# The second experts' weights: one transfer of 12 KB runs a tile in place of three of 2 KB and 1 KB runs

## The chip, the cores and the metric

One core of one Trainium2 chip. The metric is the device time of the whole program in microseconds (us); the kernel before was run three times, and its median is 5924.18 us.

## The reference, cut to what matters

A tower of feed-forward blocks with routed experts and of attention blocks, on 4096 tokens of width 256. The change touches only the second kind of feed-forward block, which occurs twice (`_L1_ffn_ref`). Each token goes to the one expert of 32 whose gate is highest, scaled by that gate's sigmoid:

```python
def _L1_ffn_ref(hidden_states, gate_w, ..., routed_gate_w, routed_up_w, routed_down_w):
    H, I, E = 256, 512, 32
    x = hidden_states.reshape(-1, h)
    shared_out = _swiglu(x, shared_gate_w, shared_up_w, shared_down_w)
    logits = x @ gate_w
    topk_ids = jnp.argmax(logits, axis=-1)
    scores = jax.nn.sigmoid(jnp.max(logits, axis=-1))[:, None]
    xs = x * scores
    ...
    g = _grouped_mm(sorted_x, routed_gate_w, tokens_per_expert)
    u = _grouped_mm(sorted_x, routed_up_w, tokens_per_expert)
    d = _grouped_mm(jax.nn.silu(g) * u, routed_down_w, tokens_per_expert)
    ...
    return (shared_out + routed_out).reshape(b, s, h)
```

An expert has a gate and an up matrix of 256 x 512 and a down matrix of 512 x 256, all float32: 512 KB each, 1.5 MB (1.573 million bytes) together.

## The kernel before, in words

The program runs its blocks one after another, with a barrier between them: first experts (names that begin with a), attention (b), first experts again (c), second experts (d), another attention (e), second experts again (f). A block of second experts has three phases: a norm (dn, fn), a routing phase (dr, fr) that computes the shared expert and lays out the tokens, and the experts' phase (de, fe) in `experts1_phase`, which alone uses the code that is changed.

Routing puts the tokens into NS1 = 4096/128 + 32 = 64 slots of 128 rows, each slot for one expert; unused rows and slots point to dummy rows. `experts1_phase` runs over these 64 tiles. Every engine has its own program, and semaphores tie them together; a name such as `s_y` counts the tiles that have come so far.

- SyncE (`tile`, L944): reads the tile's expert number from `eid`, waits until the tile four earlier has gone through its down product (`s_y`, lag WR = 4), and issues the three loads of that expert's matrices (L949 to L951) into slot `u % WR` of `wg`, `wu` and `wd`. Each load adds 16 to the slot's semaphore `s_w`. In `wg` and `wu` a partition holds 2 rows (HC = 2) of 512 floats, which are 2 KB runs in DRAM; in `wd` it holds 4 rows (FC = 4) of 256 floats, 1 KB runs.
- GpSimd (L960 to L987): issues the indirect gathers of the tiles' rows, six tiles ahead (LEAD = RING - 2), and the indirect scatters of the results. Its order per tile n is written out: gather n + 6, wait for the result's copy (`s_yc`), wait until the scatter of tile n - 1 has landed (`s_o`, L984), scatter n (L985). So scatters never overlap each other, and a gather stands behind the scatter of the tile before.
- VectorE: scales the gathered rows into `gs` (L1058), and multiplies silu(gate) by up into `h` (L1067).
- TensorE (`tile`, L1007): transposes tile n + 1 (L1010, helper at L995), waits for the weights of tile n (L1011), the 16 gate and the 16 up products of 128x128 by 128 columns (L1017), then the 8 matmuls of 256 columns of the down product of tile n - 1 (L1003).
- ScalarE: copies the transposed rows out of PSUM (L1032), silu (L1045), and copies the result into one of four `y` buffers (L1038); a buffer is free when the scatter four tiles earlier has landed.

SyncE's loads and GpSimd's gathers and scatters run on the same 16 DMA engines, through two queues: q1 (SyncE) and q0 (GpSimd). After the last tile SyncE waits for all scatters and reads the routed rows back (`r`, L957), and VectorE adds them to x.

The loads and the wait for them are:

```python
for dst, src in ((wg, "L1_rg"), (wu, "L1_ru"), (wd, "L1_rd")):
    sp.dma_start(dst[:, u % WR], D[src][ds(e, 1)].rearrange("e (c p) f -> p (e c) f", p=P)
                 ).then_inc(s_w[u % WR], 16)
...
pe.wait_ge(s_w[u % WR], 48 * quarter(k, u))
```

The first experts' phases (ae, ce) load each expert's matrices in one transfer of 3 KB a partition (`L0_w`, L684).

Of the kernel before, what the change touches and what calls it, by code (L numbers as in the profile page):

```python
# [16 lines left out]
P = 128  # L17
B, S, H = 2, 2048, 256
# [5 lines left out]
HC = H // P  # L24
EPS = 1e-5
NEG_BIG = -3.0e38
ds = bass.ds
# [6 lines left out]
E1, F1 = 32, 512  # L34
# [27 lines left out]
def rings_of(eng, count, body, ring=RING, start=0):  # L62

    i0, i1 = start // ring, count // ring
    for u in range(ring):
        body(start + u, u, i0 + 1, start + u, None)
    if i1 - i0 > 2:
        with eng.Fori(i0 + 1, i1 - 1) as i:  # L70
            for u in range(ring):
                body(i * ring + u, u, i + 1, None, None)
    for u in range(ring):
        body(count - ring + u, u, i1, None, ring - u)


def after(eng, sem, n, lag, first, count=lambda k: k):

    if first is None or first >= lag:
        eng.wait_ge(sem, count(n - lag + 1))  # L80


def moved(first, d):

    return None if first is None else first + d
# [818 lines left out]
WR = 4  # L904
# [6 lines left out]
def experts1_phase(nc, name, D, C, x, stats, rows, routed, eid, idx, ident, s_g, s_o, run):  # L911
# [3 lines left out]
    g0, o0 = run * 16 * (NS1 // RING), run * 16 * (NS1 // NY1)  # L915
    FC = F1 // P
    with Scope(nc, name) as sc:
        wg, wu = (sc.sb(n, [P, WR, HC, F1]) for n in ("wg", "wu"))
        wd = sc.sb("wd", [P, WR, FC, H])
        g = sc.sb("g", [P, RING, ROW1])  # L920
        gs = sc.sb("gs", [P, 4, H])
        xe = sc.sb("xe", [P, 2, HC, P])
# [1 line left out]
        h = sc.sb("h", [P, 2, FC, P])  # L924
# [3 lines left out]
        psG = sc.ps("psG", [P, 2, FC, P])  # L928
        psU = sc.ps("psU", [P, 2, FC, P])
        psY = sc.ps("psY", [P, 2, BLK])  # L930
        s_w = [sc.sem(f"w{u}") for u in range(WR)]
# [4 lines left out]
        s_gs, s_xt, s_xe, s_gp, s_up, s_sg, s_hh, s_y, s_yc = (  # L936
            sc.sem(n) for n in ("gs", "xt", "xe", "gp", "up", "sg", "hh", "y", "yc"))

        quarter = lambda k, u: k * (RING // 4) + (u // 4 + 1 - RING // 4)

        with nc.Block() as block:  # L941

            @block.sync
            def _(sp):  # L944
                def tile(n, u, k, first, last):
                    e = sp.value_load(eid[0:1, ds(n, 1)], min_val=0, max_val=E1 - 1)

                    after(sp, s_y, n, WR, first)
                    for dst, src in ((wg, "L1_rg"), (wu, "L1_ru"), (wd, "L1_rd")):  # L949
                        sp.dma_start(dst[:, u % WR], D[src][ds(e, 1)].rearrange("e (c p) f -> p (e c) f", p=P)  # L950
                                     ).then_inc(s_w[u % WR], 16)  # L951

                rings_of(sp, NS1, tile)
                for u in range(NY1):
                    sp.wait_ge(s_o[u], o0 + 16 * (NS1 // NY1))
                for q in range(NQ1):
                    sp.dma_start(r[:, q * (NT // NQ1) * H:(q + 1) * (NT // NQ1) * H].rearrange("p (t h) -> p t h", h=H),  # L957
                                 routed[q * (T // NQ1):(q + 1) * (T // NQ1), :].rearrange("(t p) h -> p t h", p=P)
                                 ).then_inc(s_r[q], 16)
# [29 lines left out]
            @block.tensor  # L989
            def _(pe):  # L990
                def transposes(n, u, first):
                    pe.wait_ge(s_gs, n + 1)
                    after(pe, s_xe, n, 2, first)
                    for c in range(HC):
                        last = nc.tensor.transpose(psX[:, u % 2, c * P:(c + 1) * P],  # L995
                                                   gs[:, u % 4, c * P:(c + 1) * P], ident[:])
                    last.then_inc(s_xt, 1)

                def down(n, u, first):
                    pe.wait_ge(s_hh, n + 1)  # L1000
                    after(pe, s_yc, n, 2, first)
                    for m in range(FC):
                        last = nc.tensor.matmul(psY[:, u % 2, 0:H], h[:, u % 2, m, :], wd[:, u % WR, m, :],  # L1003
                                                start=(m == 0), stop=(m == FC - 1))
                    last.then_inc(s_y, 1)

                def tile(n, u, k, first, last):  # L1007

                    if last != 1:
                        transposes(n + 1, (u + 1) % RING, moved(first, 1))  # L1010
                    pe.wait_ge(s_w[u % WR], 48 * quarter(k, u))  # L1011
                    pe.wait_ge(s_xe, n + 1)
                    after(pe, s_hh, n, 2, first)
                    for ps, w, done in ((psG, wg, s_gp), (psU, wu, s_up)):
                        for m in range(FC):
                            for c in range(HC):
                                mm = nc.tensor.matmul(ps[:, u % 2, m, :], w[:, u % WR, c, m * P:(m + 1) * P],  # L1017
                                                      xe[:, u % 2, c, :], start=(c == 0), stop=(c == HC - 1))
                        mm.then_inc(done, 1)
                    if first != 0:  # L1020
                        down(n - 1, (u - 1) % RING, moved(first, -1))

                transposes(0, 0, 0)
                rings_of(pe, NS1, tile)
                down(NS1 - 1, RING - 1, None)

            @block.scalar
# [1062 lines left out]
def macaron_kernel(nc, D, out):  # L2090
# [10 lines left out]
    with Scope(nc, "all") as sc:  # L2101
# [23 lines left out]
        def experts1(n, run):  # L2125
            with Scope(nc, n) as f:
                idx, eid, dest = f.sb("idx", [P, NS1], I32), f.sb("eid", [P, NS1], I32), f.sb("dest", [P, NT], I32)
                with Scope(nc, n + "f") as g:
                    xnT, logits = g.sb("xnT", [P, HC, T]), g.sb("logits", [P, NT * E1])
                    wg, wu, wd = g.sb("wg", [P, HC, F1]), g.sb("wu", [P, HC, F1]), g.sb("wd", [P, F1 // P, H])  # L2130
                    s_w = g.sem("w")
                    loads = (wg[:], D["L1_sg"]), (wu[:], D["L1_su"]), (wd[:], D["L1_sd"])
                    norm_phase(nc, n + "n", x, stats, xnT, C["ident"], rows1, ROW1, D["L1_gate"], E1, logits, loads, s_w)
                    route1_phase(nc, n + "r", D, C, x, xnT, logits, rows1, eid, idx, dest, wg, wu, wd, s_w)
                experts1_phase(nc, n + "e", D, C, x, stats if run == 0 else None, rows1, routed, eid, idx, C["ident"], s_g1, s_o1, run)
# [44 lines left out]
def by_chunk(a):  # L2180

    return a.reshape(-1, P, a.shape[-1]).transpose(1, 0, 2)


def lay_out(I):
    D = {"L0_x": I["L0_attn_x"].reshape(T, H)}
    D["L0_gate"] = by_chunk(I["L0_ffn_gate_weight"].T)
    D["L0_ebias"] = I["L0_ffn_e_bias"]
    for k, n in (("sg", "shared_gate"), ("su", "shared_up"), ("sd", "shared_down")):
        D["L0_" + k] = by_chunk(I["L0_ffn_" + n].T)  # L2190
    up = [I["L0_ffn_" + n].transpose(0, 2, 1).reshape(E0, HC, P, F0).transpose(0, 2, 1, 3).reshape(E0, P, HC * F0)
          for n in ("w1", "w3")]
    D["L0_w"] = np.concatenate(up + [I["L0_ffn_w2"].transpose(0, 2, 1)], 2)
    for n in "qkv":
        D["L0_w" + n] = by_chunk(I["L0_attn_W" + n].T)
    D["L0_bqk"] = np.concatenate([I["L0_attn_b" + n].reshape(HC, P).T for n in "qk"], 1)
    D["L0_bv"] = I["L0_attn_bv"]
    wo = np.zeros((NHEAD, VW, H), np.float32)
    wo[:, :DH] = I["L0_attn_Wo"].T.reshape(NHEAD, DH, H)
    wo[0, DH] = I["L0_attn_bo"]  # L2200
    D["L0_wo"] = by_chunk(wo.reshape(NHEAD * VW, H))
    D["L1_gate"] = by_chunk(I["L1_ffn_gate_w"])
    for k, n in (("sg", "shared_gate_w"), ("su", "shared_up_w"), ("sd", "shared_down_w")):
        D["L1_" + k] = by_chunk(I["L1_ffn_" + n])
    for k, n in (("rg", "routed_gate_w"), ("ru", "routed_up_w"), ("rd", "routed_down_w")):
        D["L1_" + k] = I["L1_ffn_" + n]
    for n in ("q1", "q2", "k1", "k2", "v", "c"):
        D["L1_w" + n] = by_chunk(I["L1_attn_W" + n])
    heads = (np.arange(P) // (2 * VW))[:, None] + 2 * (np.arange(B * NHEAD // 2) % (NHEAD // 2))[None, :]
    D["L1_lam"] = np.stack([I["L1_attn_" + n][heads].reshape(P, -1) for n in ("lq1", "lq2", "lk1", "lk2")], 1)  # L2210
    D.update(constants())
    return {n: np.ascontiguousarray(a) for n, a in D.items()}
# [15 lines left out]
```

## Time and profile before

| what | value |
|---|---|
| three runs | 5935.9, 5924.18, 5909.79 us (median 5924.18) |
| span of the profiled execution, the only time given of it | 5916.1 us, mean granted TensorE clock 0.916 |
| TensorE matmul, weight load | 5058.1 us (85%), 2711.9 us (46%) |
| VectorE, ScalarE, GpSimd | 57%, 43%, 31% |
| DMA | 659.28 MB, mean 111 GB/s; SyncE's queue q1 27.0% of 16 engines, GpSimd's q0 13.2% |
| loads of the second experts | 64 a phase and matrix, 512.0 KB each; gate 4.7 and 4.9, up 5.9 and 5.9, down 7.3 and 7.5 us to landing (de, fe) |

Busy times are shares of the whole span and of stages with different limits. "To landing" is from the start of the issuing instruction to the last of its completions. DMA shares are the time that packets took, as a share of 16 engines in the window asked for.

### The profile page before, as it was taken

What the parts mean: (1) busy time and instruction counts of PE and PEld (TensorE: products, weight loads), DVE (VectorE), ACT (ScalarE), POOL (GpSimd) and SP (SyncE); (2) the same over time, 40 slices, a digit from 0 to 9 for tenths busy, and PEclk for the clock granted to TensorE, in tenths of its full rate; (3) what the DMA queues carried; (4) which work ended last, traced back from release to release, by engine and by line L of the source; (5) the groups of instructions that cost most, each with busy time, mean ns of one, the idle gap of its engine ahead of it and who ended that gap; (6) DMA issues with size and microseconds to landing.
All of it is one profiled execution on the core that took longest, in us unless ns stands there. A gap on an engine that the chain in (4) does not pass through costs nothing. (4 is left out here: it accounts for less than half of the span.)

```text
span 5916.1 us, 82750 instructions
## 1 busy us (share of the span) xinstructions
PE 5058.1 (85%) x29088; PEld 2711.9 (46%) x29088; DVE 3390.4 (57%) x6345; ACT 2567.7 (43%) x5102; POOL 1828.3 (31%) x1800
## 2 busy tenths in 40 slices
PE   6566489999978566499987999999999999799996
PEld 3455333333325455357973333333333333255896
DVE  7511468887846721241119788878888878343111
ACT  2311217776662311132215176766766766513221
POOL 2388311111101288534331122222222222104332
PEclk9778779999989687699998899999999999889998
DMA  3476561222213277606986411221221221120798
GB/s 107 116 148 149 138 171 33 62 58 68 62 53 104 76 156 151 149 26 212 330 269 198 108 37 40 63 49 40 64 47 40 64 48 40 55 69 1 267 318 268
DMA packets 503528, 659.28 MB, mean 111 GB/s; under 512 B 147310, under 2 KB 358318, under 8 KB 497998
## 3 DMA queue, kind: packets, MB, share of 16 engines
q1 hardware_dynamic: 370158, 500.99, 27.0%
q0 software_dynamic: 133056, 154.15, 13.2%
q8 instruction: 192, 3.15, 0.2%
q14 instruction: 122, 1.00, 0.1%
HBM read 489.33 MB, written 164.20 MB: 110 GB/s over the span
## 5 line engine op out<-in xcount | busy, mean ns | idle before, releaser
L1724 DVE TENSOR_REDUCE ea_mx<-ea_psA 128x1 f32<-128x512 f32 (+3 forms) x2304 | 1373.9, 653 | 242.0 <-PE ea_psA L1585 144.1
L1706 ACT ACTIVATE ea_pr<-ea_psB 128x512 f32<-128x512 f32 (+3 forms) x2560 | 1198.9, 535 | 567.4 <-PE ea_psB L1608 557.7
L1585 PE MATMUL ea_psA<-ex_kx,ex_qx 99*128 99x512 bf16 (+3 forms) x2560 | 868.4, 357 | 20.2 <-DVE ea_mx L1724 13.3
L1608 PE MATMUL ea_psB<-ex_qx,ex_kx 99*128 99x512 bf16 (+3 forms) x2560 | 846.2, 349 | 0.0
L1724 DVE TENSOR_REDUCE ba_mx<-ba_psA 128x1 f32<-128x512 f32 (+3 forms) x1152 | 686.2, 653 | 144.3 <-PE ba_psA L1585 95.6
L1706 ACT ACTIVATE ba_pr<-ba_psB 128x512 f32<-128x512 f32 (+3 forms) x1280 | 601.5, 536 | 288.9 <-PE ba_psB L1611 155.5
L1625 PE MATMUL ea_psO<-ea_pr,ea_vx 128*32 128x512 f32 (+3 forms) x5120 | 603.5, 543 | 20.9 <-POOL ea_pr L1554 14.0
L1585 PEld LDWEIGHTS ea_psA<-ex_kx,ex_qx 99*128 99x128 bf16 x2560 | 250.3, 98 | 551.8 <-DVE ea_mx L1724 427.8
L1585 PE MATMUL ba_psA<-bx_kx,bx_qx 108*128 108x512 bf16 (+3 forms) x1280 | 443.5, 364 | 7.8 <-PEq L1146 4.5
L1608 PE MATMUL ba_psB<-bx_qx,bx_kx 108*128 108x512 bf16 (+3 forms) x1280 | 424.9, 349 | 14.6 <-DMA bx_qx<-ba_mT 14.4
L1608 PEld LDWEIGHTS ea_psB<-ex_qx,ex_kx 99*128 99x128 bf16 x2560 | 246.5, 98 | 310.3 <-ACT ea_pr L1706 141.0
L1554 POOL TENSOR_SCALAR_AFFINE_SELECT ea_pr<-ea_pr 128x512 f32<-128x512 f32 x256 | 162.7, 638 | 633.7 <-ACT ea_pr L1706 633.5
L1625 PE MATMUL ba_psO<-ba_pr,ba_vx 128*32 128x512 f32 (+3 forms) x2560 | 300.3, 541 | 2.1 <-ACT ba_osb L1696 2.1
L1542 POOL DMA_DIRECT2D ex_qx<-ea_mT x192 | 106.8, 563 | 485.3 <-DVE ea_mT L1746 485.3
L1585 PEld LDWEIGHTS ba_psA<-bx_kx,bx_qx 108*128 108x128 bf16 x1280 | 126.0, 99 | 280.6 <-DVE ba_mx L1724 207.5
L716 POOL DMA_INDIRECT acc<-ce_y,c_idx x128 | 204.8, 1600 | 43.7 <-issue 36.0
L716 POOL DMA_INDIRECT acc<-ae_y,a_idx x128 | 204.4, 1597 | 43.9 <-issue 35.3
L1625 PEld LDWEIGHTS ea_psO<-ea_pr,ea_vx 128*32 128x32 f32 x5120 | 102.2, 108 | 242.6 <-ACT ea_pr L1706 183.5
L1588 PE MATMUL ea_psA<-all_cb 128*128 128x128 bf16 x1024 | 206.1, 225 | 0.0
L793 DVE TENSOR_TENSOR ae_h<-ae_sg,ae_psH 128x256 f32<-128x256 f32 x64 | 26.9, 421 | 302.2 <-ACT ae_sg L774 302.2
L793 DVE TENSOR_TENSOR ce_h<-ce_sg,ce_psH 128x256 f32<-128x256 f32 x64 | 26.9, 421 | 299.8 <-ACT ce_sg L774 299.8
L1608 PEld LDWEIGHTS ba_psB<-bx_qx,bx_kx 108*128 108x128 bf16 x1280 | 123.9, 98 | 139.3 <-ACT ba_pr L1706 59.5
(528 smaller groups left out, 8260.9 us busy)
## 6 DMA issues: line engine op xcount, KB each, us to landing
de_wg<-in_L_rg SPq DMA_DIRECT2D x64, 512.0 KB, 4.7
de_wu<-in_L_ru SPq DMA_DIRECT2D x64, 512.0 KB, 5.9
de_wd<-in_L_rd SPq DMA_DIRECT2D x64, 512.0 KB, 7.3
fe_wg<-in_L_rg SPq DMA_DIRECT2D x64, 512.0 KB, 4.9
fe_wu<-in_L_ru SPq DMA_DIRECT2D x64, 512.0 KB, 5.9
fe_wd<-in_L_rd SPq DMA_DIRECT2D x64, 512.0 KB, 7.5
ae_w<-in_L_w SPq DMA_DIRECT2D x64, 384.0 KB, 3.6
ce_w<-in_L_w SPq DMA_DIRECT2D x64, 384.0 KB, 3.8
```

The lines of the kernel that those rows point to most:

```text
L716: nc.gpsimd.indirect_dma_start(out=acc[a], out_offset=column(n, a), in_=y[:, n % RING, a, :], in_offset=None, bounds_check=bound, oob_is_e ...
L793: nc.vector.tensor_tensor(h[:, u % 2, :], sg[:, u % 2, :], psH[:, u % 2, 1, :], ALU.mult).then_inc(s_hh, 1)
L1542: pool.dma_start(qx[MR:MR + 3, s, hh, t0 * P:(t0 + tc) * P].rearrange("l (t q) -> l t q", q=P), mT[hh * 3 * tc:(hh + 1) * 3 * tc, k, :]).t ...
L1554: nc.gpsimd.affine_select(own, own, [[0, HV], [1, P]], ALU.is_ge, 0.0, base=0, channel_multiplier=-1).then_inc(s_pm, 1)
L1585: last = nc.tensor.matmul(psA[:, slot, at:at + n], qx[0:KB, s, hh, t * P:(t + 1) * P], kx[0:KB, s, hh, k:k + n], start=True, stop=not diag)
L1588: last = nc.tensor.matmul(psA[:, slot, at + n - P:at + n], C["identb"], C["maskA"], start=False, stop=True)
L1608: last = nc.tensor.matmul(psB[:, slot, off:BLK], kx[0:KB, s, hh, kt * P:(kt + 1) * P], qx[0:KB, s, hh, Q * BLK + off:(Q + 1) * BLK], start ...
L1625: last = nc.tensor.matmul(psO[hh * VW:(hh + 1) * VW, off:BLK], vx[:, s, kt, vcol:vcol + VW], pr[:, j % 4, hh, off:BLK], start=(kt == 0), s ...
L1706: nc.scalar.activation(pr[:, j % 4, hh, off:BLK], psB[:, exp_slot(n), off:BLK], ACT.Exp).then_inc(s_exp, 1)
L1724: v.tensor_reduce(out, src, AX.X, ALU.max).then_inc(s_ar, 1)
```

## The change

The host lays an expert's three matrices out side by side: for each expert and partition 3072 floats (12 KB), first the two rows of the gate matrix, then the two of the up matrix, then the four of the down matrix. In SBUF the three tensors `wg`, `wu` and `wd` become views of one tensor `w` of the same size. SyncE issues one transfer per tile, and TensorE waits for 16 per load in place of 48. Nothing else differs.

```diff
-        wg, wu = (sc.sb(n, [P, WR, HC, F1]) for n in ("wg", "wu"))
-        wd = sc.sb("wd", [P, WR, FC, H])
+        w = sc.sb("w", [P, WR, 3 * HC * F1])
+        at = lambda u, part: w[:, u, part * HC * F1:(part + 1) * HC * F1]
+        wg, wu = ([at(u, part).rearrange("p (c f) -> p c f", c=HC) for u in range(WR)] for part in range(2))
+        wd = [at(u, 2).rearrange("p (m h) -> p m h", m=FC) for u in range(WR)]
...
-                    for dst, src in ((wg, "L1_rg"), (wu, "L1_ru"), (wd, "L1_rd")):
-                        sp.dma_start(dst[:, u % WR], D[src][ds(e, 1)].rearrange("e (c p) f -> p (e c) f", p=P)
-                                     ).then_inc(s_w[u % WR], 16)
+                    sp.dma_start(w[:, u % WR], D["L1_w"][ds(e, 1)].rearrange("e p f -> p (e f)")).then_inc(s_w[u % WR], 16)
...
-                        last = nc.tensor.matmul(psY[:, u % 2, 0:H], h[:, u % 2, m, :], wd[:, u % WR, m, :],
+                        last = nc.tensor.matmul(psY[:, u % 2, 0:H], h[:, u % 2, m, :], wd[u % WR][:, m, :],
...
-                    pe.wait_ge(s_w[u % WR], 48 * quarter(k, u))
+                    pe.wait_ge(s_w[u % WR], 16 * quarter(k, u))
...
-                    for ps, w, done in ((psG, wg, s_gp), (psU, wu, s_up)):
+                    for ps, own, done in ((psG, wg, s_gp), (psU, wu, s_up)):
...
-                                mm = nc.tensor.matmul(ps[:, u % 2, m, :], w[:, u % WR, c, m * P:(m + 1) * P],
+                                mm = nc.tensor.matmul(ps[:, u % 2, m, :], own[u % WR][:, c, m * P:(m + 1) * P],
...
-    for k, n in (("rg", "routed_gate_w"), ("ru", "routed_up_w"), ("rd", "routed_down_w")):
-        D["L1_" + k] = I["L1_ffn_" + n]
+    rows = [I["L1_ffn_routed_" + n].reshape(E1, -1, P, I["L1_ffn_routed_" + n].shape[-1]).transpose(0, 2, 1, 3).reshape(E1, P, -1)
+            for n in ("gate_w", "up_w", "down_w")]
+    D["L1_w"] = np.concatenate(rows, 2)
```

## Rows read from the trace of the kernel before

**Rows 1.** Chain that ended last, phase fe: start us, us, what.
```profile
5514.97 1.79 PE fe_psG L1017 x16
...
5520.49 1.79 PE fe_psG L1017 x16
...
5631.50 6.65 DMA routed<-fe_y,f_idx
5638.94 4.88 DMA routed<-fe_y,f_idx
...
5829.42 5.11 DMA routed<-fe_y,f_idx
```
**Rows 2.** Waits from 5500 to 5910 us: waiter, releaser, us, times, longest.
```profile
POOL routed L985 <- DMA routed<-fe_y,f_idx: 203.9, 59, 6.4
...
PE fe_psX L995 <- DVE fe_gs L1058: 22.4, 11, 10.9
```
**Rows 3.** Windows: length, busy us of PE, PEld, DVE, ACT, POOL; clock, DMA, GB/s.
```profile
2730.00:2780.00 50.00, 50.00 (x383) 47.70 (x382) 10.00 (x20) 11.35 (x28) 15.75 (x16) 1.00 0.99 334
...
2980.00:3030.00 50.00, 48.76 (x370) 45.42 (x370) 9.29 (x19) 11.69 (x27) 17.50 (x18) 1.00 0.95 314
...
5680.00:5730.00 50.00, 47.78 (x355) 44.16 (x354) 8.84 (x18) 10.73 (x26) 18.19 (x18) 1.00 0.97 317
```
**Rows 4.** Line L985 (the scatters) from 5630 to 5835 us.
```profile
DMA to landing us min/median/max: 4.0/5.0/6.6
```
**Rows 5.** Timeline, scatters and last result copies: start us, us, engine, line.
```profile
3088.80 0.37 ACT L1038 COPY de_y<-de_psY 128x256 f32<-128x256 f32 x1 [2.92 <-PE de_psY L1003]
...
3095.38 0.98 POOL L985 DMA_INDIRECT routed<-de_y,d_idx  x1 [2.19 <-DMA routed<-de_y,d_idx]
...
5520.97 1.04 POOL L985 DMA_INDIRECT routed<-fe_y,f_idx  x1 [12.09 <-ACT fe_y L1038]
...
5874.73 0.37 ACT L1038 COPY fe_y<-fe_psY 128x256 f32<-128x256 f32 x1 [2.92 <-PE fe_psY L1003]
...
5879.53 0.98 POOL L985 DMA_INDIRECT routed<-fe_y,f_idx  x1 [2.20 <-DMA routed<-fe_y,f_idx]
5882.70 0.98 POOL L985 DMA_INDIRECT routed<-fe_y,f_idx  x1 [2.19 <-DMA routed<-fe_y,f_idx]
```
**Rows 6.** DMA queues from 5530 to 5850 us: packets, MB, share of 16 engines.
```profile
q1 hardware_dynamic: 60541, 88.66, 81.9%
q0 software_dynamic: 5177, 14.17, 15.3%
```
**Rows 7.** DMA queue q1 from 236 to 245 us: loads of 3 KB runs (ae_w).
```profile
q1 hardware_dynamic: 961, 2.65, 81.2%
```
**Rows 8.** DMA queue q1 from 1755 to 1764 us: a store of 8 KB rows (yT).
```profile
q1 hardware_dynamic: 144, 1.05, 28.4%
```
**Rows 9.** DMA queue q1 from 3520 to 3530 us: loads of 8 KB rows (ea_rec).
```profile
q1 hardware_dynamic: 192, 1.05, 45.6%
```
**Rows 10.** Timeline, first gate products of tiles 1 and 63 in de and fe.
```profile
2729.80 1.95 PE L1017 MATMUL de_psG<-de_xe,de_wg 128*128 128x128 f32 x16
...
3083.30 1.95 PE L1017 MATMUL de_psG<-de_xe,de_wg 128*128 128x128 f32 x16
...
5514.81 1.95 PE L1017 MATMUL fe_psG<-fe_xe,fe_wg 128*128 128x128 f32 x16
...
5869.23 1.95 PE L1017 MATMUL fe_psG<-fe_xe,fe_wg 128*128 128x128 f32 x16
```
**Rows 11.** Timeline, the start of phase de: first loads, the second gather.
```profile
2715.58 0.42 SPq L950 DMA_DIRECT2D de_wg<-in_L_rg  x1
...
2716.60 0.42 SPq L950 DMA_DIRECT2D de_wd<-in_L_rd  x1
2717.04 1.06 POOL L969 DMA_INDIRECT de_g<-rows,d_idx  x1 [0.30 <-issue]
2717.80 0.38 SPq L950 DMA_DIRECT2D de_wg<-in_L_rg  x1
```

## The prediction

> **What bounds the kernel now.** I read the page first, then the chain of waits, then the two stages that the change touches, by waits, windows, timeline and DMA share. TensorE is busy 85% of the span on the page, but that is an average over stages; the edit is used only in the two stages of the second experts, "de" (2715 to 3119 us) and "fe" (5499 to 5902 us). There are 64 tiles in each, so what matters is what sets a tile's time there.
>
> Early in a stage it is TensorE: a window of 50 us holds 50.00 us of matmul [rows 3], and the chain runs through the gate, up and down products, one tile each 5.52 us (5514.97 to 5520.49) [rows 1]. Later the chain leaves TensorE: from 5631.50 to 5829.42 it is made of 35 scatters of results, one behind the other [rows 1], because GpSimd waits for the landing of scatter n-1 before it issues scatter n (L984 to L985): 59 such waits, 203.9 us [rows 2]. TensorE feels it through the gathers, which stand in the same GpSimd program: 11 waits for gathered rows, 22.4 us, of which 10.9 is the stage's start [rows 2]. The matmul share of a 50 us window falls to 47.78 in fe and 48.76 in de [rows 3].
>
> What makes a scatter slow is the weight traffic. Beside the loads it lands in a median of 5.0 us (4.0 to 6.6) [rows 4]; at the stage's end, with no load left, scatters follow each other every 3.17 us (5879.53, 5882.70) [rows 5]. GpSimd needs 0.79 us from a landing to the next start: 5631.50 + 6.65 = 5638.15, and the next begins at 5638.94 [rows 1]. So a scatter alone takes 3.17 - 0.79 = 2.38 us, and 5.0 - 2.38 = 2.62 us is waiting behind weights. The period of the chain is 5.0 + 0.79 = 5.79 us by the median; from the first scatter at 5520.97 to the last at 5882.70 there are 63 steps of 5.74 [rows 5]. The stage loses because 5.74 is just above TensorE's 5.52, and by no more.
>
> The 16 DMA engines stand at the same brim. In 320 us of fe the weight queue takes 81.9% and GpSimd's 15.3% [rows 6]. Weights: 0.819 x 16 x 320 / 88.66 = 47.3 engine-us per MB; a tile of 1.573 MB is 74.4, over 16 engines 4.65 us. GpSimd's: 88.66 / 1.573 = 56.4 tiles, 0.153 x 320 / 56.4 = 0.87 us. Together 5.52 us a tile: full.
>
> **The change, part by part.**
>
> *Run length.* The same bytes, but 128 pieces of 12 KB in place of 512 of 2 KB and 512 of 1 KB. No row shows 12 KB. The nearest by route are the first experts' loads, 3 KB a partition into 128 partitions: 0.812 x 16 x 9 / 2.65 = 44.1 engine-us per MB [rows 7], so 4.34 us a tile. The nearest by size are stores of 8 KB rows: 0.284 x 16 x 9 / 1.05 = 38.9 [rows 8], so 3.83 us. I take 3.95, nearer the second, since what a piece costs shrinks with their count, and keep 3.83 and 4.34 for the range. Farthest are loads of 8 KB rows: 0.456 x 16 x 10 / 1.05 = 69.5 [rows 9], 6.83 us a tile; with GpSimd's 0.87 that is 7.70, and 126 steps would cost 126 x (7.70 - 5.74) = 247 us. Those go into 32 partitions each (L1500 to L1502), the weights into 128 as the 3 KB loads do, so I keep that end out of the range. The Trainium skill ("DMA: Bandwidth & Descriptors", Where 436 GB/s comes from) puts the ceiling of the 16 engines at 435 GB/s; an estimate by that page is 1.573 MB / 435 GB/s = 3.62 us, by which the start below would cost 0.7 us a stage less and the time would be 1.3 us lower.
>
> *What follows for the chain.* A drain of 3.95 in place of 4.65 shortens the wait behind it by 0.70: landing 4.3, period 4.3 + 0.79 = 5.09, below 5.52. With 4.34 it is 4.69 + 0.79 = 5.48, barely below. The DMA engines then have 5.52 - 3.95 - 0.87 = 0.70 us a tile to spare. In both cases TensorE's 5.52 holds to the end, and TensorE is late next. Worth in the middle: de's tile 1 starts at 2729.80 and its tile 63 at 3083.30, fe's at 5514.81 and 5869.23 [rows 10]. That is 353.50 and 354.42 for 62 tiles; 62 x 5.52 = 342.24. Gain 11.26 + 12.18 = 23.4 us.
>
> *Tail.* The last scatters run late because the chain lags. Without a lag tile 62's scatter starts when its copy ends, 5874.73 + 0.37 = 5875.10, and the last 3.17 later at 5878.27; now it is 5882.70: 4.4 us. In de 3088.80 + 0.37 + 3.17 = 3092.34 against 3095.38: 3.0 [rows 5]. Gain 7.4 us.
>
> *Start.* TensorE transposes tile 1 before tile 0's products (L1010, L1017), so the stage begins when gather 1 lands. Now gather 1 (2717.04) is issued before tile 1's first transfer (2717.80), behind tile 0's load alone [rows 11]. SyncE needs 1.20 us from tile 0's last issue (2716.60) to tile 1's first; with one issue a tile, tile 1's whole load goes out at 2715.58 + 1.20 = 2716.78, before gather 1. Gather 1 then waits for one load more, 3.95, less the 0.70 by which the first is shorter: 3.2 us a stage, a loss of 6.4 in all. Its ends: nothing, if the gather is served between pieces, and 4.34 each.
>
> *At nothing:* SyncE issues one transfer a tile and not three, off the path between tiles. The wait for 16 in place of 48 asks for the same bytes; a load is issued three tiles (16.6 us) before its use, and the view of [rows 2] lists no wait of TensorE for weights. If that cover went, a drain of 3.95 would stand in the open at each tile. The matmuls keep count and shape and read other addresses of the same partitions. The array in DRAM is laid out on the host.
>
> **Sum.** 23.4 + 7.4 - 6.4 = 24.4 us less than the profiled span of 5916.1 gives 5891.7. That span is 8.1 below the median of the three runs (5924.18), so by the median 5899.8 us, 0.41% faster. A measurement of this kernel can tell about 0.5% from no change; the three runs spread over 26 us.
>
> **Rivals.**
> A. *No start cost*: the gather slips between pieces. 23.4 + 7.4 = 30.8, so 5893.4. For it: few pieces are queued when the first gathers come. Against it: beside loads, GpSimd's transfers wait 2.62 us now.
> B. *Little shortens.* The weights' 4.65 us hold stalls beside gathers that may go by time and not by piece; the 3 KB loads at 44.1 against 47.3 show a gain of 7% for twice the run. If the landing falls by just 0.1, that is 63 x 0.1 x 2 = 12.6, less 6.4: 5918.
> C. *The scatter meets a whole load.* All 1.5 MB now enter the queue at once, where before three transfers came 0.5 us apart and a scatter could get in between. It lands at 2.38 + 3.95 = 6.33, the period is 7.12, and 63 x (7.12 - 5.74) x 2 = 174 us are lost: 6098. It decides from a landing of 4.95 on: above that the kernel is slower than now, below 4.73 TensorE binds. For it: the worst scatter of [rows 4], 6.6, waits 6.6 - 2.38 = 4.22, nearly a whole load of 4.65, so what is ahead in the queue drains first. Against it: a scatter that waits falls behind the loads' phase, towards the 0.70 us a tile in which the queue is empty, a gap that is missing now. The Trainium skill (same page, Queues, rings and completion order) says that an engine goes round its queues and drains a whole packet, up to 64 descriptors, before it switches. By that rule the 8 pieces of a load on an engine could go as one unit where now a third of a load does, and the time would be that of C; the trace agrees as far as the median wait of 2.62 is longer than a third of 4.65.
> D. *The pieces are cut smaller than 12 KB.* At 3 to 8 KB apiece the prices above hold, so it falls into the forecast or B.
>
> **Chances.** Forecast 0.52, A 0.13, B 0.20 (D lies in the forecast and B), C 0.15. Under 5894.6 (0.5% faster): most of A and, by the spread of the runs, a sixth of the forecast, 0.20. Above 5953.8: C, 0.15. Within: 0.65. The range takes in the forecast with its bounds (5893.4, and 5924.2 - 30.8 + 2 x 4.34 = 5902), A and B, both widened by the spread: 5886 to 5935. It leaves out C and a few hundredths at the lower end.
>
> **What would show it.** Right: the weight queue's share in fe's middle falls from 81.9% to about 70%, the scatter's median landing from 5.0 to at most 4.7, windows hold 50.00 us of matmul up to the last tiles, tile 1 to tile 63 takes about 342 us, the last scatter starts some 3 us after the one before it with no five in a row at 3.17, and a stage's first matmul comes about 3 us later after SyncE's first issue than now. A weight queue still above 78% is B; scatters that land in 5 to 7 us while that share falls are C. A wait of TensorE for weights, or a tile in the middle that takes longer than 5.52 without any wait, would make the whole reading wrong.

## The result and the profile after

| | before | after |
|---|---|---|
| median of eight runs each, us | 5923.93 (5909.79 to 5939.61) | 5955.51 (5941.48 to 5970.55) |
| ratio, 95% interval | | 1.0059 (1.0045 to 1.0073) |
| span of the profiled execution, us | 5916.1 | 5939.7 |
| mean granted TensorE clock | 0.916 | 0.917 |
| first scatter to last, de, us | 359.43 | 373.55 |
| first scatter to last, fe, us | 361.73 | 377.86 |

The kernel became slower by 31.6 us, where 24.4 less was forecast; 5955.5 lies above the predicted range of 5886 to 5935. The two bottom rows say where: the 63 steps from a stage's first scatter to its last take 14.1 us longer in de and 16.1 in fe, 30.2 together, which is nearly all of the slowdown. (Of before, the ends of both spans and fe's start stand in [rows 5]; de's first scatter starts at 2735.95.) The profiled spans differ by only 23.6, since the rest of the program varies too: without these two stretches the profiled executions of all kernels of this study take between 5177 and 5231 us, 5195 before and 5188 after.

The rows after that answer to those of before. Landing of the scatters, line L985, first the stretch of [rows 4] in fe, then 2800 to 3080 us in de:

```profile
DMA to landing us min/median/max: 2.5/5.4/7.2
...
DMA to landing us min/median/max: 2.5/5.4/9.0
```

The median rose from 5.0 to 5.4, where I had forecast 4.3. The spread tells more: some scatters now land in 2.5 us, as if there were no weights, and others in 7 to 9. Against 2.5 alone and 4.32 us for a whole load (worked out below), the scatter sometimes meets a whole load and sometimes none.

The DMA queues from 5530 to 5850 us (packets, MB, share of 16 engines), which answer to [rows 6]:

```profile
q1 hardware_dynamic: 7786, 85.09, 73.1%
q0 software_dynamic: 4986, 13.65, 12.4%
```

The weights did become cheaper: 0.731 x 16 x 320 / 85.09 = 44.0 engine-us per MB against 47.3, or 4.32 us a tile against 4.65. The packets fell from 60541 to 7786. With both queues the engines are busy for 85.5% and no longer for 97%. The resource that stood at the brim got room, and yet the stage slowed down. The windows (length, busy us of PE, PEld, DVE, ACT, POOL; clock, DMA share, GB/s), de early and late, then fe, against [rows 3]:

```profile
2740.00:2790.00 50.00, 50.00 (x384) 47.70 (x383) 8.88 (x18) 11.50 (x28) 16.53 (x16) 1.00 0.89 324
2990.00:3040.00 50.00, 48.01 (x356) 45.66 (x356) 8.34 (x17) 10.74 (x25) 18.72 (x18) 0.97 0.85 307
5690.00:5740.00 50.00, 45.58 (x330) 43.41 (x329) 7.15 (x14) 10.14 (x24) 14.83 (x15) 0.93 0.78 280
```

TensorE loses 4.4 us of 50 in fe, where it lost 2.2. Cut into 5 us, the last of these windows shows how:

```profile
5695.00:5700.00 5.00, 5.00 (x42) 4.80 (x41) 0.76 (x2) 1.34 (x3) 2.06 (x2) 1.00 0.84 317
5700.00:5705.00 5.00, 1.43 (x7) 0.93 (x5) 0.00 (x0) 0.37 (x1) 1.68 (x2) 0.99 0.86 318
5705.00:5710.00 5.00, 4.15 (x20) 4.15 (x21) 1.00 (x2) 0.38 (x2) 0.39 (x1) 0.50 0.56 212
5710.00:5715.00 5.00, 5.00 (x31) 4.75 (x31) 1.04 (x2) 1.05 (x3) 2.92 (x3) 0.82 0.17 54
5715.00:5720.00 5.00, 5.00 (x40) 4.74 (x39) 1.04 (x2) 0.83 (x3) 1.21 (x2) 1.00 0.87 314
```

TensorE stands idle for 4.42 us, until 5705.85, because the rows of the next tile are not there; the DMA engines are busy all the while, with weights. Then its granted clock is 0.50, which is the 1.2 GHz level, through the window from 5705 and into the next (0.82 over it), and back at 1.00, the 2.4 GHz level, from 5715 on. And since SyncE issues loads by TensorE's counts, the DMA engines run empty after the gap: a share of 0.17. That is where 2.5 us landings come from (the scatter issued at 5710.89 lands in 2.5, the one before it took 7.1), and how engines with room to spare go with a slower stage. Who waits, from 5506 to 5930 us:

```profile
POOL routed L985 <- DMA routed<-fe_y,f_idx: 221.1, 60, 6.5
...
PE fe_psX L995 <- DVE fe_gs L1058: 33.5, 9, 12.7
```

These are the two lines of [rows 2], longer: GpSimd waits 17.2 us more for its own scatters, TensorE 11.1 us more for gathered rows. No wait of TensorE for weights has appeared. The chain that ended last, fe:

```profile
5525.85 1.74 PE fe_psY L1003 x8
5527.62 0.38 ACT fe_y L1038
...
5528.27 6.46 DMA routed<-fe_y,f_idx
...
5535.56 6.08 DMA routed<-fe_y,f_idx
...
5542.44 3.81 DMA routed<-fe_y,f_idx
```

In [rows 1] TensorE's products carried the chain until about 5630; now scatters carry it from the first one of the stage, at 5528.27. The starts and ends of the stages in the timeline (start us, us, engine and line):

```profile
2723.97 3.74 SPq L951 DMA_DIRECT2D de_w<-in_L_w  x4
...
2733.09 3.03 PE L1017 MATMUL de_psG<-de_xe,de_w 128*128 128x128 f32 x16
...
2737.96 1.95 PE L1017 MATMUL de_psG<-de_xe,de_w 128*128 128x128 f32 x16
...
2744.11 1.03 POOL L985 DMA_INDIRECT routed<-de_y,d_idx  x1 [10.94 <-ACT de_y L1038]
...
3103.80 1.95 PE L1017 MATMUL de_psG<-de_xe,de_w 128*128 128x128 f32 x16
...
3109.30 0.37 ACT L1038 COPY de_y<-de_psY 128x256 f32<-128x256 f32 x1 [2.92 <-PE de_psY L1003]
...
3117.66 0.98 POOL L985 DMA_INDIRECT routed<-de_y,d_idx  x1 [2.20 <-DMA routed<-de_y,d_idx]
...
5522.12 1.95 PE L1017 MATMUL fe_psG<-fe_xe,fe_w 128*128 128x128 f32 x16
...
5893.32 1.95 PE L1017 MATMUL fe_psG<-fe_xe,fe_w 128*128 128x128 f32 x16
...
5898.82 0.37 ACT L1038 COPY fe_y<-fe_psY 128x256 f32<-128x256 f32 x1 [2.92 <-PE fe_psY L1003]
...
5906.13 0.98 POOL L985 DMA_INDIRECT routed<-fe_y,f_idx  x1 [2.19 <-DMA routed<-fe_y,f_idx]
```

Tile 1 to tile 63 takes 365.8 us in de (2737.96 to 3103.80) and 371.2 in fe (5522.12 to 5893.32), against 353.5 and 354.4 in [rows 10]. The first product comes 9.12 us after SyncE's first issue (2723.97 to 2733.09), 8.45 before: the start lost 0.7 us, not 3.2 (in fe, by the same two rows, 9.99 against 9.20).

### The profile page after: what moved, and what is told of

It reads as the page before. It is cut to its first block and busy times, and to the rows that moved or that the text cites. A ratio compares the mean times of both kernels' runs of the same rounds, so it can differ in the third digit from the quotient of the medians.

```text
span 5939.7 us, 82238 instructions
## 1 busy us (share of the span) xinstructions
PE 5053.2 (85%) x29088; PEld 2718.0 (46%) x29088; DVE 3387.0 (57%) x6345; ACT 2565.8 (43%) x5102; POOL 1829.5 (31%) x1800
```

## The experiments

Two theories stood at first. *Burst* (also called order theory below, later transfer theory): a scatter waits for what one issue has put ahead of it, so one large transfer hurts and several small ones help. *Piece*: a long piece holds a DMA engine between two of GpSimd's packets. Its later form, *drain*: the wait follows the time that a tile's weights take on the DMA engines, however they are issued. (Two expectations put a 12 KB piece at 0.46 us; by the measured drain, with 128 pieces over 16 engines, it is 4.32 / 8 = 0.54.) All kernels are derived from the changed one unless it is said; "step" is the time from the first scatter in the timeline to the last, over 63, and drain is what the weight queue's row gives per tile.

| kernel | transfers a tile, KB each | pieces | median us | ratio to before, 95% | step de, fe us | drain us |
|---|---|---|---|---|---|---|
| before | 3, 512 | 2, 2, 1 KB | 5923.93 | 1 | 5.71, 5.74 | 4.65 |
| after | 1, 1536 | 12 KB | 5955.51 | 1.0059 (1.0045 to 1.0073) | 5.93, 6.00 | 4.32 |
| e2_one_2k | 1, 1536 | 2 KB | 6002.33 | 1.0129 (1.0110 to 1.0148) | 6.30, 6.55 | 4.75 |
| e3_one_4k | 1, 1536 | 4 KB | 5924.54 | 0.9995 (0.9977 to 1.0012) | 5.85, 6.03 | 4.48 |
| e5_late_12k | 1, 1536 | 12 KB | 5944.70 | 1.0039 (1.0024 to 1.0053) | 5.99, 6.02 | 4.29 |
| e4_two_8k_4k | 2, 1024 and 512 | 8, 4 KB | 5944.69 | 1.0040 (1.0025 to 1.0055) | 5.70, 5.84 | 4.42 |
| e1_three_4k | 3, 512 | 4 KB | 5906.82 | 0.9978 (0.9964 to 0.9992) | 5.60, 5.59 | 4.40 |
| e6_spread_three_4k | 3, 512 | 4 KB | 5910.96 | 0.9982 (0.9970 to 0.9994) | 5.72, 5.63 | 4.53 |
| e8_six_2k | 6, 256 | 2 KB | 5890.24 | 0.9949 (0.9930 to 0.9968) | 5.51, 5.52 | 4.55 |
| e11_before_in_six | 6, 256 | 2, 2, 1 KB | 5893.54 | 0.9960 (0.9947 to 0.9973) | 5.50, 5.51 | 4.68 |
| e7_four_loads | none after tile 3 | | 5895.03 | 0.9955 (0.9939 to 0.9971) | 5.48, 5.48 | 0 |
| e9_two_scatters_12k | 1, 1536 | 12 KB | 5893.47 | 0.9953 (0.9939 to 0.9968) | 5.46, 5.46 | 4.46 |
| e10_four_by_32_12k | 4, 384 | 12 KB | 6284.97 | 1.0627 (1.0600 to 1.0654) | 8.57, 8.48 | 7.01 |
| e12_eight_by_16_12k | 8, 192 | 12 KB | 6698.44 | 1.1310 (1.1272 to 1.1349) | 11.46, 11.19 | 9.95 |

Every ratio is to runs of the kernel before on the same chip, whose medians were 5923.9, 5919.7 (e1 to e4), 5917.4 (e5 to e8) and 5918.2 (e9 to e12). Steps are of one profiled execution, ratios of many. As differences from the kernel before they agree within about 10 us for most kernels; for e3 and e4 the steps and the medians differ by some 20 us in opposite ways (for e10 by 14, for e12, whose profiled execution was 39 us below its median, by 75), and e3's twelve times alone run from 5899.6 to 5937.5.

**Number of transfers, piece size held: e1, e2, e3, e4.**

```diff
# e1_three_4k
+for a, b in ((0, 1024), (1024, 2048), (2048, 3072)):
+    sp.dma_start(w[:, u % WR, a:b], D["L1_w"][ds(e, 1)][:, :, a:b].rearrange("e p f -> p (e f)")
+                 ).then_inc(s_w[u % WR], 16)
-pe.wait_ge(s_w[u % WR], 16 * quarter(k, u))
+pe.wait_ge(s_w[u % WR], 48 * quarter(k, u))
# e2_one_2k (e3_one_4k the same with 3 in place of 6)
+sp.dma_start(w[:, u % WR].rearrange("p (t f) -> p t f", t=6),
+             D["L1_w"][ds(e, 1)].rearrange("e t p f -> p (e t) f")).then_inc(s_w[u % WR], 16)
-    D["L1_w"] = np.concatenate(rows, 2)
+    D["L1_w"] = np.concatenate(rows, 2).reshape(E1, P, 6, -1).transpose(0, 2, 1, 3)
# e4_two_8k_4k
+for a, b in ((0, 2048), (2048, 3072)):
```

> The changed layout, but an expert loaded by three transfers again (gate, up, down), in pieces of 4 KB a partition. Burst theory (the changed kernel is slower because all 1.5 MB enter the queue by one issue, and a scatter behind it waits for all of it): three issues 0.5 us apart let scatters in as before, and the pieces cost less, so scatters land in a median of 5.0 us or less and the time is 5895 to 5925 us. Piece theory (it is slower because a 12 KB piece of 0.46 us holds an engine between two of GpSimd's packets): a 4 KB piece takes a third of that, so the loss shrinks to about a third, 5930 to 5940 us.

> One transfer an expert as in the changed kernel, but laid out in DRAM so that it moves in pieces of 2 KB, six a partition. Burst theory: the whole load still enters at once, and drains no faster than in 12 KB pieces, so at least the changed kernel's 5955 us, up to 5990. Piece theory: the pieces are those of the kernel before or near them, so the time is near its 5924 us, 5912 to 5932.

> One transfer an expert, in pieces of 4 KB, three a partition. Burst theory: about the changed kernel's time, 5945 to 5965 us, and slower than the three transfers of 4 KB by 20 us or more. Piece theory: the same as the three transfers of 4 KB within 10 us, 5930 to 5940 us.

> The changed layout, loaded by two transfers: gate and up together in pieces of 8 KB, then down in pieces of 4 KB. Burst theory: two thirds of a load enter at once, so between the three transfers and the one, 5915 to 5945 us. Piece theory: the 8 KB pieces set it, 5940 to 5950 us.

e1 gave 5906.8, e2 6002.3, e3 5924.5, e4 5944.7. The strongest of these is e2: its drain is nearly that of the kernel before (4.75 against 4.65 us a tile), and it is 82.6 us slower than that kernel's runs beside it (6002.33 - 5919.69). Piece theory put it below 5932; burst theory had the direction, but at most 5990. Its queues from 5600 to 5900 us, and its scatters in the stretch of [rows 4]:

```profile
q1 hardware_dynamic: 36049, 72.32, 72.8%
q0 software_dynamic: 4273, 11.69, 10.7%
```

```profile
DMA to landing us min/median/max: 2.5/5.9/8.5
```

As in the changed kernel, the engines are less busy (83.5%) and the scatters land later. e1 has three issues and 4 KB pieces: its drain (4.40) is the changed kernel's (4.32) within 2%, its three issues are those of the kernel before, and it is faster than both; its scatters in that stretch:

```profile
DMA to landing us min/median/max: 3.8/4.7/6.0
```

e4 lies inside both forecasts and decides nothing. e3 fell below the range of both theories: by burst theory a single transfer of 4 KB pieces should have been slow. Its landings look like those of the changed kernel (longest 7.3 in this stretch), its median time does not, and I have no explanation for that.

**Time of the issue: e5 and e6.**

```diff
# e5_late_12k
-after(sp, s_y, n, WR, first)
+if first is None or first >= WR:
+    sp.wait_ge(s_gp, n - 1)
# e6_spread_three_4k: e1's three transfers, and ahead of the second and third
+if part and (first is None or first >= WR):
+    sp.wait_ge((s_gp, s_up)[part - 1], n - 1)
```

> The same single transfer of 12 KB pieces as the changed kernel, but SyncE issues it after the gate product of the tile before last instead of after the down product four tiles back, some 2 us later in the tile. Order theory (a scatter waits for the part of a load that one issue has put ahead of it): the scatter and the gather of the tile are now issued ahead of the load, the scatter's median landing falls from 5.2 to about 4, the 62 tiles between the second and the last take 342 to 348 us in each stage, and the kernel comes to 5890 to 5915 us. Drain theory (the wait follows the share of the DMA engines that the weights take, 4.3 us a tile, whenever they are issued): the landing stays at 5.2, the 62 tiles at 366 and 371, the kernel at 5945 to 5960.

> Three transfers of 4 KB pieces a tile as in the run before last of that size (5906.8 us), but apart: the gate's after the down product four tiles back, the up's after the gate product, the down's after the up product of the tile before last, each 1 to 2 us behind the other. Order theory: no scatter has more than about a third of a load ahead of it, the median landing falls below 4.5 (longest below 5.5), TensorE binds to the end, 62 tiles take 342 to 345 us, and the kernel comes to 5890 to 5903 us. Drain theory: the weights take the same 4.4 us a tile, the landing stays at 4.9 and the kernel at 5903 to 5912.

e5 gave 5944.7 and e6 5911.0. They missed the order theory's numbers by 30 and 8 us and came out where the drain theory had them (e5 at its lower end). e5, gathers then scatters of 5580 to 5830 us:

```profile
DMA to landing us min/median/max: 3.2/5.1/8.8
...
DMA to landing us min/median/max: 3.5/5.3/7.8
```

The gather, 5.7 us in the changed kernel, lands in 5.1, but the scatter is where it was. Scatters of e6 in the stretch of [rows 4]:

```profile
DMA to landing us min/median/max: 4.3/5.0/5.9
```

Nothing lands early any more and nothing late: there is always a third of a load in the way. So when in the tile a load is issued does not matter, or not lastingly. A likely reason, which is argued from the 5 us windows above and was not tried by itself: the scatter chain is slower than TensorE in e5, TensorE waits for the gathers that stand in that chain, and the loads go out by TensorE's counts, so loads and scatters drift back into the same relation. What remains of the order theory is the size of one transfer, which e8 and e11 test.

**The floor: e7.**

```diff
-                rings_of(sp, NS1, tile)
+                for n in range(WR):
+                    tile(n, n, 1, n, None)
-                    pe.wait_ge(s_w[u % WR], 16 * quarter(k, u))
+                    pe.wait_ge(s_w[u % WR], 16)
```

> Only the weights of a stage's first four tiles are loaded, and the later tiles compute with them: 60 of 64 loads a stage are left out. It gives the floor that the weights' traffic stands above. Both theories: the scatter lands in about 2.4 us, TensorE binds from the second tile to the last, 342 to 345 us, and the kernel takes 5885 to 5900 us. If it takes more than 5910, something other than the weights' traffic holds the stage above TensorE, and both theories are short of a term.

5895.0 us, as both expected. Scatters in the stretch of [rows 4], and the window of fe:

```profile
DMA to landing us min/median/max: 2.4/2.5/2.5
```

```profile
5690.00:5740.00 50.00, 50.00 (x381) 47.60 (x381) 8.58 (x18) 11.29 (x27) 18.65 (x18) 1.00 0.15 47
```

Without weights a scatter takes 2.5 us (I had worked out 2.38 for a scatter alone), TensorE binds, and the kernel is 0.45% faster than before. All that the weights' traffic costs the kernel before is 22 us (5917.4 - 5895.0); nothing done to the loads can win more than that, as far as runs tell.

**Smaller transfers: e8 and e11.** e8 is e1 with six slices of 512 floats and a wait for 96. e11 is not derived from the change, but is the kernel before with each matrix in two halves:

```diff
+half = dst.shape[2] // 2
+for j in range(2):
+    sp.dma_start(dst[:, u % WR, j * half:(j + 1) * half],
+                 D[src][ds(e, 1), j * half * P:(j + 1) * half * P].rearrange("e (c p) f -> p (e c) f", p=P)
+                 ).then_inc(s_w[u % WR], 16)
-pe.wait_ge(s_w[u % WR], 48 * quarter(k, u))
+pe.wait_ge(s_w[u % WR], 96 * quarter(k, u))
```

> Six transfers of 2 KB pieces a tile in place of one of 12 KB, issued back to back. The single transfer of 2 KB pieces took 6002 us, so this one differs from it by the number of issues alone. Order theory: a scatter gets in between issues that are 0.5 us apart, its median landing is 4.7 to 5.2 and not 6.2, and the kernel takes 5905 to 5935 us. Drain theory (768 pieces of 2 KB cost 4.75 us a tile whatever the issues): 5985 to 6010 us.

> The kernel before with its three separate matrices and its pieces of 2 KB and 1 KB, but each matrix in two transfers: six a tile of 256 KB. Transfer theory: smaller transfers help without any new layout; mean landing 4.75 to 4.85, the kernel takes 5890 to 5910 us, 0.2 to 0.4% below the kernel before. Drain theory (pieces and bytes are the same, so is the load on the DMA engines): equal to the kernel before within 0.1%, 5912 to 5924.

5890.2 and 5893.5: both at the floor (the intervals overlap that of e7), faster than before and after, and for e8 better than either theory had it. e8 against e2 is the largest difference: 2 KB pieces in both, six issues for one, 112 us less; but e2's pieces also lie in another order in DRAM, so its expectation's "by the number of issues alone" isn't quite so. The clean pair is e11 against the kernel before: the very same pieces of the same arrays, six transfers for three, 24.6 us less (5918.16 - 5893.54). Drain theory had no change there. The queues of e8, 5530 to 5850 us:

```profile
q1 hardware_dynamic: 50098, 91.21, 82.5%
q0 software_dynamic: 5344, 14.64, 14.3%
```

its scatters in the stretch of [rows 4], and its window of fe:

```profile
DMA to landing us min/median/max: 4.0/4.8/6.0
```

```profile
5690.00:5740.00 50.00, 50.00 (x383) 47.70 (x382) 9.11 (x18) 11.53 (x28) 18.59 (x18) 1.00 0.97 335
```

The weight queue takes a larger share than in [rows 6] (82.5 against 81.9%), the window's DMA share is 0.97 as in [rows 3], and TensorE is never idle. Full DMA engines were not what held the stage. The serial chain is still there; GpSimd's waits of e8 from 5500 to 5930 us:

```profile
POOL routed L987 <- DMA routed<-fe_y,f_idx: 197.5, 61, 6.5
```

GpSimd still stands behind 61 landings. But until the last dozen tiles a scatter starts at most 5.1 us after its result's copy has ended, where in the kernel before that lag grows to 15 and more. That the gathers, issued six tiles ahead, cover the small lag is argued from the order of GpSimd's program; the windows show that TensorE does not feel it.

**What turns a late scatter into time: e9.**

```diff
+routed2 = nc.dram_tensor(name + "_routed2", (T + P, H), F32, kind="Internal").ap()
-if n or run:
-    pool.wait_ge(s_o[(n - 1) % NY1], o0 + 16 * ((n - 1) // NY1 + 1))
+if n > 1 or run:
+    pool.wait_ge(s_o[(n - 2) % NY1], o0 + 16 * ((n - 2) // NY1 + 1))
-out=routed, out_offset=column(n), in_=y[:, n % NY1, :], in_offset=None,
+out=(routed, routed2)[n % 2], out_offset=column(n), in_=y[:, n % NY1, :], in_offset=None,
```

> The changed kernel with its single transfer of 12 KB pieces, but the scatters of odd tiles go to a second array, and a scatter waits for the landing of the one two tiles back instead of the one before, so two can be under way. It leaves out the reading back of the routed rows: the rows read at the stage's end are those that the gathers read, so the output has no routed part. Chain theory (the load only matters because each scatter stands behind the landing of the one before; a stage takes 63 times the mean landing plus 0.79 us): GpSimd waits for landings almost no more, TensorE binds from the second tile to the last (342 to 348 us for those 62 steps), and the kernel takes 5885 to 5905 us though a single scatter may still land after 5 us or later. Rival (a whole load in front of the gathers holds TensorE by itself): 62 steps stay above 358 us and the kernel at 5930 to 5955.

5893.5 us: the floor, with the change's own load of 1.5 MB untouched. Scatters in the stretch of [rows 4], then GpSimd's waits from 5500 to 5930 us:

```profile
DMA to landing us min/median/max: 6.5/8.2/9.2
```

```profile
POOL routed L986 <- ACT fe_y L1039: 113.5, 32, 12.7
POOL fe_routed L986 <- ACT fe_y L1039: 97.3, 31, 4.5
```

A scatter now lands after 8.2 us, the slowest of all the kernels that load at full rate, and it costs nothing: GpSimd waits for the results' copies, and hardly ever for a landing (`fe_routed` is the second array). So the load does harm only through the rule that a scatter stands behind the landing of the one before. (The rows at the end are read from a wider array here, so the tail is not quite that of the others.)

**The same pieces in narrow transfers: e10 and e12.** I wanted smaller transfers with 12 KB pieces, and the partitions were the only axis left to cut.

```diff
+for a in range(0, P, 32):
+    sp.dma_start(w[a:a + 32, u % WR], D["L1_w"][ds(e, 1)][:, a:a + 32, :].rearrange("e p f -> p (e f)")
+                 ).then_inc(s_w[u % WR], 16)
-pe.wait_ge(s_w[u % WR], 16 * quarter(k, u))
+pe.wait_ge(s_w[u % WR], 64 * quarter(k, u))
```

> The 12 KB pieces of the changed kernel, in four transfers of 32 partitions each. Transfer theory (what counts is how large one transfer is, not the piece and not the time of the issue): as with three or six transfers, mean landing of a scatter 4.7 to 4.85, 62 steps of 342 to 348 us, kernel 5890 to 5910 us. Piece theory (a 12 KB piece cannot be interrupted and holds its engine 0.46 us): like the single transfer, 5940 to 5960. By the row of 8 KB loads into 32 partitions (69.5 engine-us per MB) a tile's weights would take 6.83 us, the DMA engines would bind with 7.7 us a tile, and the kernel would take over 6100.

> The 12 KB pieces in eight transfers of 16 partitions each. Transfer theory: at least as good as six transfers, 5885 to 5905 us, unless SyncE with eight issues a tile becomes late (0.5 us apart they take 4.0 of the 5.5 us of a tile, so it should not). Piece theory: 5940 to 5960. If 16 partitions do not reach all DMA engines evenly, the weights' drain rises above 5 us a tile and the kernel above 6000.

6285.0 and 6698.4, where the 32-partition row in e10's expectation (over 6100) and the last condition of e12's had them. They say nothing for or against the transfer theory, since the drain itself grew. e10's weight queue, 5750 to 6200 us:

```profile
q1 hardware_dynamic: 10165, 83.30, 82.5%
```

That is 0.825 x 16 x 450 / 83.30 = 71.3 engine-us per MB, the price of the 32-partition loads in [rows 9] (69.5), and 7.0 us a tile. The Trainium skill ("SBUF — State Buffer", Door 1: The DMA port swizzle) says that 32 neighbouring partitions lie on 8 of the 16 ports through which the DMA engines reach that memory, and gives 189 GB/s measured for such a load; the row agrees, with 83.30 MB in 450 us, 185 GB/s.

## Why the prediction was wrong

*The reading of the kernel before held.* The chain is GpSimd's scatters, one behind the other's landing, and TensorE is late next. e9 shows the first part: with two scatters under way the wait of [rows 2] is gone and TensorE binds. The upper threshold worked out for rival C, a landing of 4.95 above which the kernel is slower than before, also held in the kernels that load at full rate with the scatters in one chain. Taking a step minus 0.79 as the mean landing in fe: e1 and e6 with 4.80 and 4.84 lie below it and are faster; e4, after, e5 and e2 with 5.05, 5.21, 5.23 and 5.76 are slower. Only e3, with 5.24 in its one profile, does not fit. The lower threshold, 4.73, is not tested by this: e8 and e11 come to 4.73 and 4.72, but their step is TensorE's own 5.52, which is how 4.73 was worked out.

*The run length was half of the gain I took.* The drain fell to 4.32 us, beside the bound of 4.34 from the 3 KB loads [rows 7], and not to the 3.95 that I put nearer the 8 KB stores [rows 8]. By the chain's sum this alone would still have made 4.67 of the landing and left TensorE binding.

*The step that failed* is "A drain of 3.95 in place of 4.65 shortens the wait behind it by 0.70." I let the scatter's wait shrink one for one with the drain of a tile, as if it were a fixed fraction of queue time. The runs show that the wait also goes by how much one transfer puts into the queue: at nearly equal drain, 4.55 to 4.75, the step in fe is 5.51 and 5.52 with six transfers (e11 and e8, where TensorE sets it), 5.74 with three (before) and 6.55 with one (e2). The edit made a step of the chain 0.26 longer in fe and 0.22 in de, and 63 x (0.26 + 0.22) = 30.2 us is nearly the loss that was measured. That the number of transfers sets the chain's length is shown by e11, and e2 says the same with its pieces in another order in DRAM; how much of the 30.2 is the merging and how much the 12 KB piece was not separated. Fewer transfers and longer pieces came in one edit, and only the second was worth something: e1, with longer pieces and still three transfers, is 0.22% faster than before.

*The middle and the tail* followed from that step. Tile 1 to 63 grew by 12.3 and 16.8 us where 23.4 less was forecast, and the tail by 1.1 where 7.4 less was forecast: by the prediction's own measure the last scatter of de is late by 3117.66 - (3109.30 + 0.37 + 3.17) = 4.8 us, before 3.0, that of fe by 5906.13 - (5898.82 + 0.37 + 3.17) = 3.8, before 4.4.

*The start* was over-sized: 0.7 and 0.8 us and not 3.2 a stage. In all, 29.1 + 1.1 + 1.5 = 31.7 us more by the profiled executions, against 23.4 + 7.4 - 6.4 = 24.4 less in the forecast.

*Rival C had the mechanism, not its size.* It was given 0.15 and 6098 us. I had every scatter meet a whole load, landing at 6.33. In fact the landings of the changed kernel are spread between 2.5 and 9.0: some scatters meet empty DMA engines, though in the gap that follows a stall of TensorE and not in the 0.70 us a tile of which I wrote "against it". The mean in fe is about 5.2. By the prediction's own signs the outcome is C: scatters that land in 5 to 7 us (median 5.4) while the weight queue's share falls (81.9 to 73.1%). What should have weighed more is the row behind it: the worst scatter of [rows 4] already waited for nearly a whole load, so the size of a load was in the landing all along. Rivals A and B both took the run length for what matters; D is out, the packets fell as the edit says.

*One transfer as one unit.* The Trainium skill ("DMA: Bandwidth & Descriptors", Queues, rings and completion order) says that an engine drains a packet of one queue before it turns to the next. One transfer as such a unit fits the changed kernel as far as its longest landing, 9.0, holds 6.5 us of waiting, more than a whole load of 4.32. It does not fit the small transfers: 256 KB drain in about 4.55 / 6 = 0.76 us, yet e8's scatters wait 4.8 - 2.5 = 2.3. The same page of the Trainium skill (Rules for kernel authors) advises to coalesce many small transfers into a large one. No run here shows a gain from that at these sizes, 192 KB and more, not even for the bytes alone: with 2 KB pieces the drain is 4.55 us a tile in six transfers and 4.75 in one, and by the time of the whole kernel six transfers of 256 KB beat one of 1536 KB by 1.1% (0.9949 against 1.0059).

*Still open:* why a smaller transfer lets scatters through sooner when a later or a spread issue does not, and why e3 is not slower than before. By its median e3 stands 17.7 us above e1 (three transfers of its 4 KB pieces) and 31.0 below the changed kernel (one transfer of 12 KB pieces), by its steps beside the changed kernel; so whether a 12 KB piece does harm of its own in a single transfer isn't settled either.

## What to carry to other kernels

A larger transfer is a longer thing to stand behind: before merging transfers, look for a serial chain of small ones on another queue, and price the merging by that chain's landing time, not by the bytes or the share of the DMA engines. Longer pieces and fewer transfers are two edits; make them apart. Where small transfers depend on each other's landing, the surest cure is to let two be under way, as then even an 8 us landing cost nothing (e9, which left out the reading back of the results; what a second array costs a complete kernel was not run); the cheapest here was to split the loads, which brought the kernel to the floor of no loads at all (e8, 0.9949; e11 without any new layout, 0.9960).

## What was unexpected of the hardware

- DMA engines that were busy for 97% of a window did not slow the stage (e8), and stages whose engines had room were slower (after, 78% in the fe window; e2, 83.5% by its queues).
- The price of a byte hardly falls beyond pieces of 3 KB: 44.0 engine-us per MB for 12 KB pieces, 44.1 for the 3 KB loads of [rows 7]. The same 12 KB pieces into 32 partitions at a time cost 71.3, and into 16 at a time, by e12's weight queue (89.2% of 650 us for 91.70 MB), 101.
- Without weights beside them the scatters land in 2.4 to 2.5 us, all of those in the stretch of [rows 4] (e7).
